# Attention with a ring of three PSUM banks for keys and values, transposed probabilities and blocks of X, and a new order of every engine's work in a step

## What is computed

```python
def _L0_xattn_ref(pcd_up, pcd_down, Wq, Wk, Wv, Wskip):
    q = jnp.einsum('oc,bcn->bon', Wq, pcd_up)
    k = jnp.einsum('oc,bcm->bom', Wk, pcd_down)
    v = jnp.einsum('oc,bcm->bom', Wv, pcd_down)
    energy = jnp.einsum('bcn,bcm->bnm', q, k) / scale
    attention = jax.nn.softmax(energy, axis=-1)
    x = jnp.einsum('bnm,bcm->bcn', attention, v)
    skip = jnp.einsum('oc,bcn->bon', Wskip, pcd_up)
    return skip + x
...
    g = jnp.einsum('bsh,ih->bsi', x, Wg)
    u = jnp.einsum('bsh,ih->bsi', x, Wu)
    h = jax.nn.silu(g) * u
    return jnp.einsum('bsi,hi->bsh', h, Wd)
...
x = x + _L0_xattn_ref(_layernorm(x, axis=-1), ctx_1024, ...)
x = x + _L0_ffn_ref(_layernorm(x, axis=-1), ...)
```

## Time and profile before

| | us |
|---|---|
| median of 3 runs (1554.44 to 1559.08) | 1557.01 |
| the profiled execution's own time | 1554.79 |
| its span, first to last instruction | 1552.8 |
| TensorE busy with matmuls | 1478.1 |
| VectorE, ScalarE, POOL busy | 794.3, 658.0, 217.5 |

### The profile page before, as it was taken

The page is one execution under the profiler, slowest core; times in us unless marked ns, Lnnn a source line. Parts: engine busy times, 40 slices in busy tenths (PEclk is TensorE's granted clock), DMA queues, the critical chain, the costliest instruction groups (busy, mean ns, idle before and its releaser), DMA issues.

```text
span 1552.8 us, 18609 instructions
## 1 busy us (share of the span) xinstructions
PE 1478.1 (95%) x6774; PEld 722.5 (47%) x6774; DVE 794.3 (51%) x1143; ACT 658.0 (42%) x1189; POOL 217.5 (14%) x281
## 2 busy tenths in 40 slices
PE   7888788999999999999999999999999999999996
PEld 5555555544444444444444444444444444444442
DVE  4666666684464463463473463563463463563340
ACT  5676766424434433433433333433433333433344
POOL 1222222101101101101101101101101101101102
PEclk9899999999999999999999999999999999999999
DMA  5121212215755746746737737737737737737748
GB/s 173 61 72 68 75 62 68 64 46 96 148 96 106 146 86 118 144 75 129 142 66 137 139 61 148 136 58 148 134 64 149 131 60 149 135 56 149 144 84 163
DMA packets 44723, 166.42 MB, mean 107 GB/s; under 512 B 6416, under 2 KB 9232, under 8 KB 40336
## 3 DMA queue, kind: packets, MB, share of 16 engines
q0 software_dynamic: 25344, 92.29, 35.9%
q1 hardware_dynamic: 19200, 73.42, 17.0%
q10 hardware_dynamic: 144, 0.26, 0.1%
HBM read 65.28 MB, written 100.66 MB: 107 GB/s over the span
## 4 chain that ended last, share of the span: by engine, by line
PE 84%; DVE 8%; issue 5%; ACT 2%; POOL 0%; POOLq 0%; ACTq 0%; DVEq 0%
PE ps L470 45%; PE ps L526 25%; PE ps L413 2%; PE ps L381 2%; PE ps L631 2%; PE ps L409 2%; PE ps L414 2%; PE ps L616 2%; PE ps L403 1%; DVE w_gu L1101 1%; DVE xt L1025 1%; DVE h_all L1012 1%; DVE stats L1000 1%; PE ps L368 1%; ACT stage L790 1%
## 5 line engine op out<-in xcount | busy, mean ns | idle before, releaser
L470 PE MATMUL ps<-xt,w_gu 128*128 128x512 f16 x3528 | 789.2, 379 | 2.2 <-ACT temps L760 2.2
L470 PEld LDWEIGHTS ps<-xt,w_gu 128*128 128x128 f16 x3528 | 345.1, 98 | 417.3 <-ACT temps L760 3.0
L526 PE MATMUL ps<-w_d_all,h_all 128*128 128x512 f16 x1920 | 440.6, 379 | 5.6 <-ACT stage L790 5.6
L790 ACT ACTIVATE stage<-ps,pow 128x512 f32<-128x512 f32 x352 | 240.6, 687 | 407.2 <-PE ps L526 390.3
L343 POOL DMA_DIRECT2D out<-stage x176 | 152.4, 866 | 1097.1 <-ACT stage L790 1097.1
L526 PEld LDWEIGHTS ps<-w_d_all,h_all 128*128 128x128 f16 (+1 forms) x1920 | 187.1, 98 | 234.5 <-ACT stage L790 10.1
L1166 DVE TENSOR_TENSOR temps<-ps,temps 128x512 f32<-128x512 f32 x42 | 29.1, 692 | 236.0 <-PE ps L470 236.0
L777 ACT CAST h_all<-temps 128x512 f16<-128x512 f32 x42 | 25.8, 613 | 132.4 <-DVE temps L1185 132.4
L1171 DVE TENSOR_TENSOR temps<-ps,temps 128x512 f32<-128x512 f32 x42 | 29.1, 692 | 95.4 <-PE ps L470 95.4
L1175 DVE TENSOR_TENSOR temps<-ps,temps 128x512 f32<-128x512 f32 x42 | 29.0, 690 | 75.7 <-PE ps L470 75.7
L1179 DVE TENSOR_TENSOR temps<-ps,temps 128x512 f32<-128x512 f32 x42 | 28.9, 689 | 75.1 <-PE ps L470 75.1
(11 more groups left out here) (108 smaller groups left out, 1295.2 us busy)
## 6 DMA issues: line engine op xcount, KB each, us to landing
out<-stage POOLq DMA_DIRECT2D x176, 512.0 KB, 5.4
grid<-grids SPq DMA_DIRECT2D x136, 256.0 KB, 5.0
raw<-packed SPq DMA_DIRECT2D x22, 512.0 KB, 4.3
stage<-x SPq DMA_DIRECT2D x13, 512.0 KB, 3.6
out<-stage SPq DMA_DIRECT2D x13, 512.0 KB, 2.6
raw_d<-packed SPq DMA_DIRECT2D x12, 512.0 KB, 8.1
w_gu<-ctx SPq DMA_DIRECT2D x16, 128.0 KB, 2.1
w_gu<-x SPq DMA_DIRECT2D x3, 512.0 KB, 3.4
```

The source lines that it names most:

```text
L470: mm = pe.matmul(bank, w_gu[e][:, wp, w, P * j:P * j + P], xt[:, xb, xp, j, cols], start=(fresh and n == 0), stop=(n == 3 * J - 1), skip_g ...
L526: mm = pe.matmul(ps[:, 6 + oh, :], h, w, start=(n == 0), stop=(n == len(products) - 1))
L790: act.activation(stage[:, t % STAGES, NOUT * oh:NOUT * oh + NOUT], ps[:, 6 + oh, :], ACT.Copy, scale=pow2[:, 10:11]).then_inc(s_stage, 1)
```

## The change

Banks 4, 5 and 7 become one ring. Every use of the three kinds (keys and values of a batch, one column half of the transposed probabilities, one block) is numbered in TensorE's order (`USES`), takes bank number n modulo 3, and waits only for the use three before it (`bank_free`). The transposed probabilities are signalled and copied out as two pieces of 128 by 512 rather than one of 128 by 1024. The normalized x has three buffers rather than two (the third lies in `raw_d`, whose first load now waits for the end of attention). Row statistics and POOL's inverse deviation run two batches ahead rather than one. The order of a step is new on TensorE, ScalarE and VectorE, and POOL's reduction over partitions stands ahead of its steps.

```diff
+def uses_of_step(i):
+    uses = [("block", u) for w in ("sums", "between") for u in blocks_of_step(i, w)]
+    if i >= 1:
+        uses += [("probs", i - 1, 1, h) for h in range(2)]
+    uses += [("block", u) for u in blocks_of_step(i, "after")]
+    if i + 1 < B:
+        uses += [("keys", i + 1)]
+    if i < B:
+        uses += [("probs", i, 0, h) for h in range(2)]
+    return uses
+
+RING = [4, 5, 7]
+        xn = [h_all[:, 0:1024], h_all[:, 1024:2048], raw_d[:, :].bitcast(F32)]
+            def bank_free(use):
+                n = NTH_USE[use] - len(RING)
+                if n < 0:
+                    return
+                kind, *of = USES[n]
+                if kind == "probs":
+                    b, f, h = of
+                    pe.wait_ge(s_prob_t_sb, 4 * b + 2 * f + h + 1)
+                elif kind == "keys":
+                    pe.wait_ge(s_vt_sb, of[0] + 1)
+                else:
+                    pe.wait_ge(s_xt_lo, NTH_UNIT[of[0]] + 1)
...
             def probs_transposed(b, f):
                 pe.wait_ge(s_prob, 2 * b + f + 1)
-                wait(pe, s_prob_t_sb, 2 * b + f)
                 for h in range(2):
+                    bank_free(("probs", b, f, h))
+                    bank = ring_bank(("probs", b, f, h))
...
+            for i in range(STEPS):
+                if i < B:
                     energies(i, 0)
+                for unit in blocks_of_step(i, "sums"):
+                    block_transposed(unit)
+                if i >= 1:
                     values(i - 1, 0)
+                for unit in blocks_of_step(i, "between"):
+                    block_transposed(unit)
+                if i < B:
+                    energies(i, 1)
+                if i >= 1:
                     probs_transposed(i - 1, 1)
+                for unit in blocks_of_step(i, "after"):
+                    block_transposed(unit)
+                if i + 1 < B:
+                    keys_values(i + 1)
+                if i >= 1:
                     values(i - 1, 1)
+                if i < B:
+                    probs_transposed(i, 0)
...
             def probs_out(b, f):
-                act.wait_ge(s_prob_t, 2 * b + f + 1)
-                act.copy(prob_t[:, f, :, :], ps_t).then_inc(s_prob_t_sb, 1)
+                for h in range(2):
+                    act.wait_ge(s_prob_t, 4 * b + 2 * f + h + 1)
+                    act.copy(prob_t[:, f, h, :], ring_bank(("probs", b, f, h))).then_inc(s_prob_t_sb, 1)
...
+            def step(i):      # ScalarE
+                for unit in blocks_of_step(i, "sums"):
+                    block_hi(unit)
+                if i < B:
                     exponentials(i, 0)
+                    normalize_probs(i, 0)
+                for unit in blocks_of_step(i, "between"):
+                    block_hi(unit)
+                if i >= 1:
                     probs_out(i - 1, 1)
+                if i % 2 == 0:
+                    for unit in blocks_of_step(i, "after"):
+                        block_hi(unit)
+                if i < B:
+                    exponentials(i, 1)
+                if i % 2 == 1:
+                    for unit in blocks_of_step(i, "after"):
+                        block_hi(unit)
+                if i + 1 < B:
+                    keys_out(i + 1)
+                if i < B:
+                    normalize_probs(i, 1)
+                if i + 1 < B:
+                    values_out(i + 1)
+                if i < B:
+                    probs_out(i, 0)
```

More of the change, by code:

```diff
@@ L49, in batch_of, with blocks_of_step @@
     return 8 * (i // 8) + i % 8 // 2 + 4 * (i % 2)
-def units_of_step(i):
+def blocks_of_step(i, which):
     k = i // 2
[L55 to L58, removed]
+    found = {
+        "sums": [(k - 2, T3), (k - 2, T4)] if i % 2 else [(k - 2, T1), (k - 2, T2)],
+        "between": [(k - 1, X21)] if i % 2 else [],
+        "after": [(k - 1, X22)] if i % 2 else [(k - 1, X11)],
+    }[which]
     return [(q, u) for q, u in found if 0 <= q < B // 2]
@@ L63 @@
 LATE = [(6, T3), (6, T4), (7, X21), (7, X22), (7, T1), (7, T2), (7, T3), (7, T4)]
-UNITS = [u for i in range(STEPS) for u in units_of_step(i)] + LATE
+UNITS = [u for i in range(STEPS) for w in ("sums", "between", "after") for u in blocks_of_step(i, w)] + LATE
 NTH_UNIT = {u: n for n, u in enumerate(UNITS)}
-UNITS_BEFORE = [sum(len(units_of_step(j)) for j in range(i)) for i in range(STEPS + 1)]
+def uses_of_step(i):
[9 more added lines that the diff above has]
+RING = [4, 5, 7]
+USES = [("keys", 0)] + [use for i in range(STEPS) for use in uses_of_step(i)]
+NTH_USE = {use: n for n, use in enumerate(USES)}
+XNS = 3
 def build(nc, x, ctx_in, att_weights, packed, grids, scales, zeros, out):
@@ L301, in inverse_deviation @@
                 par = b % 2
+                wait(pool, s_rstd[which], b)
                 pool.wait_ge(s_mv[which], b + 1)
@@ L394, in block_transposed @@
                     pe.wait_ge(s_mixed, 4 * k + u - T1 + 1)
-                pe.wait_ge(s_vt_sb, keys)
-                wait(pe, s_xt_lo, n)
+                if unit not in LATE:
+                    bank_free(("block", unit))
+                else:
+                    pe.wait_ge(s_xt_lo, NTH_UNIT[unit])
+                bank = ring_bank(("block", unit))
                 for j in range(J):
@@ L422, in _ @@
             pe.wait_ge(s_qk_sb, 1)
[L423 to L436, removed]
+            keys_values(0)
+            for i in range(STEPS):
+                if i < B:
                     energies(i, 0)
[L438 to L440 removed]
+                for unit in blocks_of_step(i, "sums"):
+                    block_transposed(unit)
+                if i >= 1:
                     values(i - 1, 0)
[L442 to L446, removed]
[L447 to L463 removed]
+                for unit in blocks_of_step(i, "between"):
[3 more added lines that the diff above has]
+                if i >= 1:
+                    probs_transposed(i - 1, 1)
+                for unit in blocks_of_step(i, "after"):
[3 more added lines that the diff above has]
+                if i >= 1:
+                    values(i - 1, 1)
+                if i < B:
+                    probs_transposed(i, 0)
             def product(e, g, w, xb, bank, fresh):
@@ L741, in down_hi @@
                     act.copy(w_d[:, 0, nib, :], src).then_inc(s_weight_hi, 1)
-            for b in range(2):
-                keys_out(b)
-                values_out(b)
-            exponentials(0, 0)
-            normalize_probs(0, 0)
-            exponentials(0, 1)
-            for i in range(1, STEPS):
-                if i == 10:
-                    step(i, lambda: plain_hi(0, 0))
-                elif i == 14:
-                    step(i, lambda: mixed_hi(0, 0))
-                else:
-                    step(i)
+            keys_out(0)
+            values_out(0)
+            for i in range(STEPS):
+                step(i)
+                if i == 9:
+                    plain_hi(0, 0)
+                elif i == 13:
+                    mixed_hi(0, 0)
             def m1_copy(n, idx):
@@ L1149, in _ @@
             }
-            step(0)
-            extremes()
+            step(0, extremes)
             for i in range(1, STEPS):
```

175 lines of the change are left out of this document (70 added, 105 removed).

## The result

The changed kernel takes 1504.7 us (median of 4 runs, 1503.71 to 1508.22) against 1558.05 in the same session: the ratio is 0.9664, with an interval from 0.9639 to 0.9689. The profiled execution took 1508.22 us, the longest of the four, of which the span is 1506.3. The forecast was 1503 (1488 to 1532).

A forecast was written before the change was run, and what follows sets the result against it. It took attention's steps 2 to 14 as bound by hand-offs through bank 7, plus clock loss. Steps 2 to 14 -55.6, steps 15 and 16 -5.6, start +3.4, hand-offs +5 from 1554.8 gave 1502, adjusted to 1503 us; range 1488 to 1532.

The forecast's parts named there:

- What bounded the kernel: Attention steps 2 to 14: no engine fills them; TensorE waits 31.5 us before blocks, 11.8 before keys and values; rest is clock.
- the bound of 18 us: Steps 2 to 14: a mean clock of 0.92 over 230.59 us loses at most 18 us.
- The walk through the step: Changed attention step, instruction by instruction: even 12.6 us, odd 14.4 with a 1.3 us stall before X22, pair 27.0.
- splitting: ScalarE's copy of 1024 columns (1.01 us) made as two of 512 (2 x 0.49) was said to cost nothing.
- The start: Before step 2: batch 0 passes both halves first, so step 2 starts at about 33 instead of 29.57, +3.4 us.
- the signs named: Expected in the trace: steps about 12.8 and 14.6 us, first product at about 229 to 234, part behind it 1266 us.
- The hand-offs: Unseen hand-offs between engines, added as 0.3 us a step over 17 steps, 5 us in all.
- the 1502 of the sum: Whole kernel: 1554.8 - 57.8 + 5 = 1502 us, before half of 2.2 was added for the median.
- rival 3: The clock keeps falling, one fall in each of 16 steps, 27 us: 1524, up to 1530 us; chance 0.12.
- Rival 2: VectorE's order bounds the steps, energies waiting for normalized x: each step 1.5 us longer, 1517 to 1525 us; chance 0.2.
- Rival 5: Slower: each of a pair's seven blocks waits 2.1 us because ScalarE's copies free banks late; 1584 us; chance 0.05.
- Rival 4: No change (within 0.3%): late weight loads in instances 0 and 1 give back the time won in attention; chance 0.03.

The follow-up runs named there:

- the second session: The changed kernel measured again, unaltered, in a later session: 1505.6 us, ratio 0.9676 to the kernel before.
- the order alone: The changed kernel with the banks of before (keys, values and all blocks in bank 7): 1565.2 us, ratio 1.0062.
- the best version: Kernel before with the three-bank ring, POOL's reduction moved, and X22 behind the rest of the second energies on TensorE: 1491.5 us, ratio 0.9588.
- the ring alone: Kernel before with the ring of three banks and halved copies, its old order, two buffers of normalized x and POOL's order kept: 1504.1 us, ratio 0.9667.
- the kernel with the start mended: Changed kernel with batch 2's row statistics moved, in step 0 alone, behind the second reciprocal: 1500.4 us, ratio 0.9638.
- ring and reduction: Kernel before with the ring and POOL's reduction moved ahead of batch 2's inverse deviation, old order kept: 1500.4 us, ratio 0.9645.

## Why the prediction was right

- **What bounded the kernel** was right: waits for one bank, and the clock's falls behind them. The seven stretches at the lower level cost about 12 us in five pairs, 2.4 a pair; the bound of 18 us for steps 2 to 14 in the forecast is consistent with that.
- **The walk through the step** was right almost to the row: 12.68 and 14.42 against 12.6 and 14.4, the gap before X22 1.13 against 1.3, steps 2 to 14 in 175.18 against 175.0, steps 15 and 16 in 21.09 against 20.9. One term of it was a little low: two copies of 512 columns take 1.07 us together where one of 1024 took 1.01, so splitting was not free, but it lay in ScalarE's idle time.
- **The start** was the term that was mis-sized: +11.3 (9.1 in the second session) for +3.4. The walk took the x of batch 2 as there when VectorE wanted it at 15.8; its statistics began at 21.9. So two of the signs named did not come: the first product at 229 to 234 us was at 237.11 (234.93 in the second session), and the last part took 1269.19 us, not 1266.
- **The hand-offs** of 0.3 us a step were not there. They stood in the sum with 5 us and hid most of the error of the start, so the total of 1503 is closer to 1504.7 than its terms deserve: that part of the agreement is luck. The profiled execution itself was 6.2 us above the 1502 of the sum, made of 7.9 for the start, 3.1 for the last part and 0.4 for the steps, less the 5. Of the 3.1 about 1.6 are a fall of the clock behind the first product (last section); the rest lies in the last 70 us of the program, without a cause shown.
- **The clock** stayed at 1.00 in steps 2 to 16, so rival 3 fell. The Trainium skill, "TensorE: Matmul & The Clock Gate", section "A second HAM failure mode: psum-queue depth-cycling", tells of a kernel that cycles through PSUM banks and whose clock swung with its small idle gaps. Here cycling through banks took the gaps away (32.96 down to 5.66 us in five pairs) and with them the swings, and the kernels with one bank for all blocks had both (granted clock 0.93 before, 0.94 for the order alone).
- **Rival 2** fell: VectorE has the normalized x ready at 106.50 for energies that start at 107.31. **Rival 5** fell: no sum waits for ScalarE's copies. Its loop was real in another place only, in the best version's 0.39 us. **Rival 4** fell with the time: in instances 0 and 1 TensorE waits for the same things as before, 1.0 and 2.2 us.
- The forecast weighed the change as a whole and did not say which part carries the gain. The runs do: the ring carries all of it and the order alone loses 10 us. With the reduction moved in both, the ring in the old order is 4 to 5 us faster than the whole change, so beside the ring the rest of the change gains nothing; by the traces it wins 0.2 us a pair and loses 5 to 8 us by the first product (237.11 and 234.93 against 229.44).

## What to carry to other kernels

Three banks that serve every short-lived tile in TensorE's own order, each waiting for the use three before it, can replace a careful interleaving: list the uses in that order and look which use three before is still open. Where a wait is left, move the producer of that one use, or put work that needs no bank in between. Test the storage and the order apart, since here a new order was thought out for what the storage alone did; and read the first steps by themselves, where a load that is late sits in front of work that is ready.

## What was not expected of the hardware

The same gap on TensorE was not always followed by a fall of the clock. In the kernel before, a gap of 2.0 us stands before the second sum in each of steps 4 to 13. In seven of them the lower level followed, as in the earlier trace rows before 121.57 with a skip term of 1.92 us behind it; in steps 6, 9 and 13 it did not, as before 106.80 with 1.02 behind it. Gaps of 1.13 to 1.2 us, one in two steps, were followed by no fall in the changed kernel's steps or in the ring alone, whose five pairs show a granted clock of 1.00. The order alone has gaps of 1.57, 1.13 and 2.0 to 3.0 us in its odd steps: a fall followed in steps 7, 9, 11 and 13 and none in step 5, and none in its even steps with 1.57 and 1.56. But in step 2 of the kernel with the start mended, waits of 0.93 and 1.64 us were followed by one.

One place can be compared in all 13 profiled executions, since its code is the same: some 30 us behind the first product TensorE waits 2.2 us for ScalarE. In ten executions the clock stayed at 1.00, in three it fell: both of the changed kernel and that of ring and reduction. The 15 us around that gap, in before and in the changed kernel:

```profile
316.71:331.71 15.00, 14.59 (x68) 6.68 (x69) 13.31 (x17) 3.80 (x6) 0.00 (x0) 1.00 0.10 37
267.11:282.11 15.00, 14.59 (x60) 6.33 (x61) 11.69 (x15) 2.69 (x5) 0.00 (x0) 0.89 0.11 37
```

TensorE is as busy, but got through 60 matmuls in place of 68, by an estimate about 1.6 us. Whether such a gap costs a fall is no property of the gap alone, and what decides it is not shown here. So the comparison of two single executions of this kernel can be off by that much.

POOL's reduction over partitions shows as 0.40 us busy, but POOL's next instruction came 6.8 to 8.3 us behind its end in the 13 traces. In the one with the start mended this next instruction's input was there at 28.92 us, the reduction ended at 30.24, and POOL began at 38.51. In the changed kernel the input came only at 36.26, so that trace alone does not show it. The cost of the reduction is in the idle time behind it, not in its own duration.
